# A recommender tower on one core: three gathers wait at other places, and the written-out order around the last two tiles' dot products is rearranged

## The reference

```python
e = jnp.stack([tbl_0[ids[:, 0]], ..., tbl_25[ids[:, 25]]], axis=1)      # 512 x 26 x 128
sd = jnp.einsum('bfd,bd->bf', e, r_dense_features)
ss = jnp.einsum('bfd,bgd->bfg', e, e)
pairs = ss[:, iu, ju]                                                   # upper triangle, k=1
h = jnp.concatenate([r_dense_features, sd, pairs, r_dense_features], axis=1)   # 607 columns
h = jnp.maximum(h @ W_top1 + b_top1, 0.0)                               # 607 x 512
h = jnp.maximum(h @ W_top2 + b_top2, 0.0)                               # 512 x 256
y = h @ W_top3                                                          # 256 x 1
```

## Time and profile before

| | us |
|---|---|
| median of 3 runs | 110.64 |
| lowest, highest | 110.51, 111.36 |
| the profiled execution, time | 110.51 |
| the profiled execution, span of the core | 108.6 |
| PE busy in the span | 104.1 (96%) |
| DVE, ACT, POOL busy | 75.6, 66.1, 60.4 |

### The profile page before, as it was taken

One profiled execution on the slowest core, in us unless ns is written; L12 is line 12 of the kernel. 1 busy time (PEld: TensorE's weight loads), 2 busy tenths in 40 slices (PEclk: granted clock), 3 DMA queues, 4 the chain that ended last, 5 costly groups with the idle time before them and its releaser, 6 DMA issues.

```text
span 108.6 us, 2787 instructions
## 1 busy us (share of the span) xinstructions
PE 104.1 (96%) x1095; PEld 92.9 (86%) x1095; DVE 75.6 (70%) x204; ACT 66.1 (61%) x134; POOL 60.4 (56%) x62
## 2 busy tenths in 40 slices
PE   6999999999999999999899989999999999998992
PEld 6865888888888888888699979999999999998991
DVE  2199999999999999999950880599339830287001
ACT  5555528978997999989450993529133671286120
POOL 7877877877777777777700577777537600000000
PEclk9999999999999999999999999999999999999999
DMA  2899999784999999821200022212201110000000
GB/s 67 220 257 219 247 217 247 178 239 74 312 306 293 281 330 290 223 62 50 48 24 9 21 51 54 56 50 54 63 9 48 48 30 0 6 0 0 0 6 1
DMA packets 5199, 12.75 MB, mean 117 GB/s; under 512 B 1833, under 2 KB 1961, under 8 KB 5186
## 3 DMA queue, kind: packets, MB, share of 16 engines
q1 hardware_dynamic: 3346, 8.83, 30.4%
q0 software_dynamic: 1792, 3.67, 13.2%
q10 hardware_dynamic: 48, 0.07, 0.2%
HBM read 12.56 MB, written 0.00 MB: 116 GB/s over the span
## 4 chain that ended last, share of the span: by engine, by line
PE 39%; DVE 33%; DMA 14%; issue 6%; SPq 3%; ACT 2%; DVEq 0%
DVE onehot L394 16%; PE dots L540 14%; DMA table<-tbl 14%; PE hidden L567 10%; DVE low L402 9%; DVE pairs L387 9%; PE hidden L584 2%; PE last_layers L584 2%; ACT high L330 2%; SPq L226 2%; PE turned L520 2%; PE turned L567 2%; PE hidden L556 2%; PE hidden L485 1%; PE last_layers L591 1%
## 5 line engine op out<-in xcount | busy, mean ns | idle before, releaser
L274 POOL DMA_INDIRECT rows<-tbl,gather_idx x56 | 57.5, 1027 | 25.6 <-issue 14.8
L394 DVE TENSOR_SCALAR onehot<-ids_h 125x512 fp32r<-125x512 f16 x98 | 35.9, 425 | 3.3 <-ACT ids_h L320 3.3
L387 DVE COPY pairs<-dots 31x128 f32<-31x128 f32 (+5 forms) x64 | 18.4, 287 | 18.3 <-PE dots L540 16.5
L314 ACT COPY pairs<-dots 31x128 f32<-31x128 f32 (+5 forms) x64 | 16.1, 252 | 14.8 <-PE dots L540 13.5
L485 PE MATMUL dots<-onehot,high 125*128 125x512 f32 (+1 forms) x66 | 24.8, 395 | 0.1
L485 PE MATMUL dots<-onehot,low 125*128 125x512 f32 (+1 forms) x66 | 23.8, 380 | 0.1
L330 ACT CAST high<-table 125x1024 fp32r<-125x1024 f32 (+2 forms) x13 | 13.1, 1004 | 8.8 <-DMA table<-tbl 8.7
L402 DVE TENSOR_TENSOR low<-table,high 125x512 fp32r<-125x512 f32 (+1 forms) x24 | 16.6, 691 | 0.4 <-ACT high L330 0.3
L540 PE MATMUL dots<-embT 128*64 128x54 f32 x512 | 15.8, 223 | 0.4 <-DVE pairs L387 0.4
L540 PEld LDWEIGHTS dots<-embT 128*64 128x64 f32 x512 | 15.3, 138 | 1.0 <-issue 0.6
L485 PEld LDWEIGHTS dots<-onehot,low 125*128 125x128 f32 x66 | 12.3, 188 | 2.9 <-DVE low L402 0.8
(11 more groups left out here) (55 smaller groups left out, 108.0 us busy)
## 6 DMA issues: line engine op xcount, KB each, us to landing
table<-tbl SPq DMA_DIRECT2D x10, 448.0 KB
wp<-w_pairs SPq DMA_DIRECT2D x2, 512.0 KB, 5.4
rows<-tbl,gather_idx POOLq DMA_INDIRECT x56, 4.3
table<-tbl SPq DMA_DIRECT2D x1, 560.0 KB
table<-tbl SPq DMA_DIRECT2D x10, 52.0 KB
wd<-w_dense SPq DMA_DIRECT2D x1, 512.0 KB, 4.7
w2s<-w SPq DMA_DIRECT2D x1, 512.0 KB, 5.2
table<-tbl SPq DMA_DIRECT2D x2, 224.0 KB
```

The lines of the kernel that those rows point to most:

```text
L274: pool.indirect_dma_start(out=rows[:, t % 2, n, :], out_offset=None, in_=tables[GATHERED_TABLES[n]][:, :], in_offset=bass.IndirectOffsetOn ...
L314: return nc.scalar.copy(dst, src)
L387: return nc.vector.tensor_copy(dst, src)
L394: nc.vector.tensor_scalar(onehot[i % STAGES][:, c, :], ids_h[:, i % ID_BUFFERS, :], float(c), None, ALU.is_equal).then_inc(onehot_ready, 1)
```

## The change

The three holds sit at other gathers: 38 waits for D0 (before: 37), 42 for D1 (44), 47 for D2 (51). In the list of steps the batches of tile 3 move later: B3.0 from before M0 to after D2, B3.1 to after M1, B3.2 and B3.3 to the end of the stretch before D3. L2.1 and R2.1, and Y1 and V1, move from behind D3 to before it.

```diff
-    HELD_BY_DOTS = {37: 1, 44: 2, 51: 3}
+    HELD_BY_DOTS = {38: 1, 42: 2, 47: 3}
...
-            D1 C1.0 B2.2 B2.3 L0.0 L0.1 R0.0 R0.1 C1.1 P1 B3.0 M0 H0
-            D2 Y0 C2.0 V0 B3.1 L1.0 L1.1 R1.0 R1.1 C2.1 P2 B3.2 M1 H1 B3.3 L2.0 R2.0
-            D3 Y1 C3.0 V1 L2.1 R2.1 C3.1 P3 M2 H2
+            D1 C1.0 B2.2 B2.3 L0.0 L0.1 R0.0 R0.1 C1.1 P1 M0 H0
+            D2 Y0 C2.0 V0 B3.0 L1.0 L1.1 R1.0 R1.1 C2.1 P2 M1 H1 B3.1 L2.0 R2.0 L2.1 R2.1 B3.2 Y1 V1 B3.3
+            D3 C3.0 C3.1 P3 M2 H2
             L3.0 R3.0 Y2 V2 L3.1 R3.1 M3 H3 Y3 V3""".split()]
```

## The result

| | before | changed |
|---|---|---|
| median, us | 110.91 (4 runs) | 115.34 (114.79 to 116.48, 4 runs) |
| ratio, 95% interval | | 1.0425 (1.0374 to 1.0476) |
| profiled execution, span | 108.6 | 113.5 |
| mean granted TensorE clock of the four runs | 1.0 in the profiled run | 0.983, 0.985, 1.0, 1.0 |

Medians and ranges take in all runs; a ratio leaves out a run that is over 1.5% above the fastest of its kernel.

What follows compares the result with a forecast made beforehand. PE's queue was taken to bound the kernel up to D3, DVE's copies after it. -0.25 (D2 earlier) + 4.17 (before D3) - 0.19 (copies) = +3.73 us on 110.51, giving 114.2; range 113.5 to 115.5.

Steps and rivals of the forecast that it cites:

- the term for PE's clock behind D3: Behind D3: the forecast sum held no clock cost for PE's idle 2.4 us; a lower clock stood only in rival B.
- rival B: Behind D3: PE idle about 2.4 us, clock falls to 1.2 GHz; +1 to +6.8 us, about 118; chance 0.07.
- The PE queue: Between D2 and D3: added PE work and exposed waits of 4.17 us, so D3 starts 3.92 us later.
- The start of D2: At D2: B3.0 leaves the place before M0, but C1.1's copy limits the gain to 0.25 us; start at 76.21.
- L2.1's wait: Before D3: L2.1 waits for the ReLU R2.0, formerly hidden by D3; +0.56 us.
- The base of 10.04: D2's end to D3's start in the kernel before: 10.04 us, read as wholly PE work.
- The placing of B3.3: Just before D3: the copy of B3.3, formerly hidden by L2.0, is exposed; +0.79 us.
- The sum of the stretch: D2's end to D3's start: 10.04 plus 4.17 us, D3 starting at 94.30 instead of 90.38.
- Behind D3: After D3: copies without V1 give -0.19 us; moving Y1 and L2.1 away gives back nothing, PE idle about 2.4 us.
- What holding the gathers is worth: nothing: At dots D1 and D2: gathers running beside dots do not slow them, so holding them gains 0 us.
- Rival A: Before D3: the nine gathers behind D2 set D3, 0.4 to 1.6 us later still; about 115.2; chance 0.13.

Runs made afterwards that it cites:

- gap filled: Changed kernel with 38 matmuls of zeros put after M2, in PE's idle gap behind D3; 114.21 us, ratio 1.0313.
- half-back pair: Changed kernel with L2.1 and R2.1 back behind D3, once with the new holds (116.12 us), once with holds 37, 44, 51 (111.89 us).
- order alone: Changed kernel's order of steps with the holds of the kernel before (37, 44, 51); 115.15 us, ratio 1.0395.
- half back, old holds: Changed kernel with L2.1 and R2.1 back behind D3 and the holds of before (37, 44, 51); 111.89 us, ratio 1.0089.
- gap half filled: Changed kernel with 14 matmuls of zeros put after M2, leaving 1.6 us idle behind D3; 114.23 us, ratio 1.0294.
- half back, new holds: Changed kernel, new holds kept, with L2.1 and R2.1 back behind D3; 116.12 us, ratio 1.0472.
- second set: Changed kernel measured again, unaltered, over six runs; 114.61 us, the four at full clock ratio 1.0317.

## Where the prediction was right, and the step that failed

**The step that failed** is the term for PE's clock behind D3. The sum has none: the gap of 2.4 us was worked out rightly, but what it does to the clock was put at nothing in the 114.2 and set aside as rival B. What the runs showed is a lower mean clock (0.983 to 0.985) in 6 of 14 runs with that gap; in the profiled one it fell to 0.50 and cost 1.51 us on L3.0 (3.53 against 2.02). That explains a part of the 1.1 us above the forecast. The forecast was built on the execution of 110.51, the lowest of before, and the median of before is 110.91: 0.4 us. The four changed runs lie 0.46 us above their two at full clock in the mean (115.49 and 115.03): that is the clock. The rest, about 0.3 us, is not explained and lies within what runs at full clock differ by (115.26 and 114.79).

**The PE queue** was right as a mechanism. At full clock the changed kernel is at 114.8 and 115.3 in the first set, at 114.0 to 114.9 in the second and at 114.2 with its gap filled, around the forecast of 114.2. From D0's start to V3 the full-clock profile takes 54.63 us (55.80 to 110.43) against 50.71 before (55.89 to 106.60): +3.92, forecast +3.73. D3 was to start 3.92 later; from D0 it does so 3.89 later in the first profile (38.38 against 34.49) and 4.05 in the second (38.54). One or two tenths are thus what two profiles of one kernel differ by, and the terms below are to be read with that.

**Its terms** partly cancel. The start of D2 came 0.15 us earlier, not 0.25: the handoff from ACT's last copy is 0.24 us, not 0.14, and D2 behind an idle moment takes 3.94 instead of 3.87, so D2's end gained 0.08. L2.1's wait was put at 0.56 and is 0.46 (89.42 to 89.88), but L2.1 behind it takes 2.05, not 1.79; L3.0, which also starts behind an idle moment, takes 2.02 at full clock. The base of 10.04 held 0.31 us of waiting for rows that I read as PE work ("wholly PE work"); in the changed kernel each batch of four is turned in 0.44 to 0.49, and B3.3 has a wait of some 0.2 us for gather 55 instead. The placing of B3.3 was put at 0.79 and is 0.72 (93.20 to 93.92), with 0.10 us from DVE's copy to D3, not 0.14. The sum of the stretch came to 14.02 against 14.21. D3 started at 93.92 in an execution that began 0.35 earlier, so 94.27 against 94.30.

**Behind D3** the copies gave 0.18 us, forecast 0.19, and Y1 and L2.1 nothing, as worked out: PE waits 2.37 us for the copies, forecast "about 2.4".

**"What holding the gathers is worth: nothing"** was right for the dots, and short for the rest: the third hold cost the kernel before 0.3 us.

**Rival A** (gathers in the lead): 55 was issued at 90.20, forecast 90.4; landing is 2.5 us. B3.3 waited for it, by 0.1 to 0.2 us, so this rival came true in its sign and not in its size; that the landing took 2.5 us and not 4.3 is what kept it small. The nine gathers keep their spacing of 1.25 us beside DVE's copies (90.20 less 80.18 is 10.02 for eight). The Trainium skill ("SBUF — State Buffer", section "SBUF: two separate sides") ties the starving of such gathers to fast copies from SBUF to SBUF; these copies read PSUM, so the trace does not speak against the page, as the prediction has it, but lies outside its warning. The half-back pair shows how near this rival was.

**Rival B** is where the failed step was left. I gave it 0.07, as a thing apart from the forecast, and priced it at about 118. It is no case of its own: it comes on top of the forecast in some runs, 2 of 4, 2 of 6, and 2 of 4 with the order alone. Such runs are 0.8 to 2 us longer than the others of their set; in the profiled one it is one half of layer 1 and no more (1.51 us), since the clock is granted again behind it. The argument "a gap of 2.4 us follows 4 us of dense dots" was no protection. What the right reading would have been: before, PE stood still for 0.4 us at most and had full clock; the change makes a gap of 2.4 us that no row covers, so a part of the runs at a lower clock belonged in the predicted time itself. The Trainium skill ("TensorE: Matmul & The Clock Gate", section "HAM oscillation") warns of idle gaps, and the traces agree with the warning: 0.50 granted after 2.37 us of rest. But the gaps of its example are longer than this one, so that page did not by itself give this rival's time, as the prediction has it; and here the mean clock stayed at 0.998 or more in 8 of 14 runs with the same 2.4 us.

## What the runs showed of the clock

The clock followed PE's idle time over all kernels of this case. Idle time of PE at its longest places, and the runs whose mean clock fell under 0.99:

| kernel | idle time of PE | runs with a lower clock |
|---|---|---|
| before, without holds (twice), third hold gone | 0.4 us | 0 of 87 |
| half back, old holds | 0.8 us before D3, 0.6 behind it | 0 of 7 |
| gap filled | 0.7 us before D3, 0.2 behind it | 0 of 6 |
| gap half filled | 0.7 us before D3, 1.6 behind it | 0 of 6 |
| changed, twice, and order alone | 0.7 to 0.8 us before D3, 2.4 behind it | 6 of 14 |
| half back, new holds | 0.81, 1.50 and 0.72 us in a row | 6 of 6 |
| new holds, old order | 1.8 and 4.8 us | 4 of 4 |

In the line of the changed kernel the same kernel on the same chip does both. What makes one run differ from the next was not told apart. In the second set the two groups lay 2 us apart, and the second microsecond stays open, since neither of those two runs has a profile; it need not be the clock, as the kernel before too has a run 2.2 us above its median at a clock of 0.999 (113.13 against 110.91). The effect went away in all 12 runs with the gap filled or half filled; if the 6 lower runs had fallen by chance among these 26, they would miss all 12 in about 1 of 77 cases, and would miss the 6 of one filling, among 20, in about 1 of 13. So the cause is well borne out for the two fillings together and less so for either alone. That a filled gap is worth its matmuls elsewhere is not shown.

## What to carry to other kernels

On an engine whose queue never runs dry, work is free only where another engine sets the pace: here behind the last dots, beside the copies. Moving it ahead of them costs its full time, uncovers the handoffs that it used to hide (0.5 us for a ReLU, 0.7 us for a placed batch), and leaves a gap in which PE can lose its clock. Before holding back transfers for the sake of an engine, compare that engine's work with and without them beside it: all dots took 3.9 us either way, and taking holds out was the only kind of edit that gained. A few short matmuls that take longer than their like elsewhere (0.57 against 0.44 us), or start later behind the group before (0.55 against 0.37 us), can be a wait in disguise: both times here it was rows that had not landed, and taking the hold away removed it.
